# Moving vector units, the early lists and the choice of experts among the chunks of a scan kernel

## The reference

```python
xn = layernorm(x)
dt = softplus(xn @ W_dt1.T @ W_dt2.T + b_dt2)         # [b, t, d]
A_bar = exp(dt * A)                                   # [b, t, d, n], n = 0..15
h = A_bar * h + (A_bar - 1) / A * xn * (xn @ W_B.T)   # along t
y = sum_n h * (xn @ W_C.T)
x = x + y + D_skip * xn
expert = argmax(softmax(layernorm(x) @ Wr + br))      # one of 8 for each token
x = x + gelu(layernorm(x) @ W1[expert] + b1[expert]) @ W2[expert] + b2[expert]
```

## Time and profile before

| | us |
|---|---|
| three runs: median (lowest, highest) | 726.48 (724.77, 732.52) |
| the profiled execution, its own time | 726.01 |
| its span in the trace | 724.3 |
| chunk 4 (first scan to the next chunk's first scan) | 52.8 |
| chunk 5 | 54.1 |
| chunk 6 | 51.9 |
| chunk 7 (to the end of its last scan) | 57.5 |
| from there to the end | 279.3 |

### The profile page before, as it was taken

The page is one execution under the profiler, slowest core; times in us unless marked ns, Lnnn a source line. Parts: engine busy times, 40 slices in busy tenths (PEclk is TensorE's granted clock), DMA queues, the critical chain, the costliest instruction groups (busy, mean ns, idle before and its releaser), DMA issues.

```text
span 724.3 us, 17510 instructions
## 1 busy us (share of the span) xinstructions
PE 682.5 (94%) x5826; PEld 574.6 (79%) x5827; DVE 538.0 (74%) x950; ACT 482.6 (67%) x1005; POOL 485.6 (67%) x616
## 2 busy tenths in 40 slices
PE   8899799999999998899998989999999999999997
PEld 7777677777787776678776778898999999977776
DVE  7799889989989989999999878887343333344441
ACT  3887999998998997899998586433232323233451
POOL 3889998998998987989989587233343434343331
PEclk9699999999999999999999799999999999999999
DMA  6787542342343243143242077711111111111010
GB/s 235 269 258 254 204 145 78 104 148 93 108 152 117 82 137 107 60 148 117 83 125 88 30 256 240 277 41 49 58 52 59 48 58 45 58 38 33 25 45 16
DMA packets 42290, 82.21 MB, mean 114 GB/s; under 512 B 4824, under 2 KB 12637, under 8 KB 42208
## 3 DMA queue, kind: packets, MB, share of 16 engines
q1 hardware_dynamic: 37600, 68.58, 28.7%
q0 software_dynamic: 4608, 12.59, 5.4%
HBM read 69.35 MB, written 13.37 MB: 114 GB/s over the span
## 4 chain that ended last, share of the span: by engine, by line
PE 58%; ACT 12%; POOL 9%; issue 7%; DVE 2%; DMA 1%; SPq 0%; POOLq 0%; ACTq 0%; DVEq 0%
PE WW L1172 16%; PE misc L1209 15%; PE WW L1055 10%; POOL w_sb L667 7%; PE YY L1093 7%; ACT w_sb L835 5%; ACT Csb L825 5%; PE misc L1204 2%; PE WW L1166 2%; DMA w_sb<-c_rows 1%; PE YY L1141 1%; PE misc L969 1%; ACT xin L805 1%; PE misc L981 1%; DVE w_sb L1336 1%
## 5 line engine op out<-in xcount | busy, mean ns | idle before, releaser
L667 POOL TENSOR_TENSOR w_sb<-w_sb,Csb 128x512 f32<-128x512 f32 x224 | 282.7, 1275 | 41.9 <-DVE w_sb L1336 37.7
L1055 PE MATMUL WW<-b_sb,xin 64*128 64x130 f32 (+2 forms) x2304 | 203.3, 293 | 23.4 <-DVE w_sb L1336 12.5
L1055 PEld LDWEIGHTS WW<-b_sb,xin 64*128 64x128 f32 x2304 | 168.4, 192 | 70.3 <-issue 30.6
L1336 DVE TENSOR_TENSOR_SCAN w_sb<-WW,hlast,w_sb 128x512 f32<-128x512 f32 x170 | 210.1, 1269 | 13.5 <-issue 6.5
L835 ACT ACTIVATE w_sb<-dt,negA 128x512 f32<-128x512 f32 x256 | 169.5, 709 | 4.0 <-DVE w_sb L1336 2.0
L916 ACT ACTIVATE dt<-WW,b1c 128x128 f32<-128x128 f32 x256 | 72.8, 387 | 129.2 <-PE WW L1172 129.0
L1093 PE MATMUL YY<-sm,w_sb 128*128 128x128 f32 x1024 | 142.4, 284 | 6.2 <-DVE row L1384 4.3
L729 POOL DMA_INDIRECT y_out<-CbX,ocol x36 | 42.6, 1184 | 142.0 <-DVE CbX L1758 137.3
L1093 PEld LDWEIGHTS YY<-sm,w_sb 128*128 128x128 f32 x1024 | 113.4, 143 | 21.2 <-issue 4.3
L825 ACT ACTIVATE Csb<-w_sb,invA 128x512 f32<-128x512 f32 x150 | 102.5, 713 | 23.2 <-POOL w_sb L667 21.5
L1209 PE MATMUL misc<-w_sb,dt 128*128 x512 | 115.7, 379 | 0.5 <-issue 0.5
(11 more groups left out here) (304 smaller groups left out, 817.7 us busy)
## 6 DMA issues: line engine op xcount, KB each, us to landing
w_sb<-c_rows SPq DMA_DIRECT2D x86, 256.0 KB, 3.3
CbX<-c_rows SPq DMA_DIRECT2D x42, 256.0 KB, 3.3
w_sb<-w_in SPq DMA_DIRECT2D x20, 512.0 KB, 5.7
token_rows<-row SPq DMA_DIRECT2D x8, 1024.0 KB, 4.6
w_sb<-w_in SPq DMA_DIRECT2D x24, 256.0 KB
...
```

Source lines behind the costliest of these rows:

```text
L667: eng.tensor_tensor(hc[g % NHC], hb_of(g), Csb[i % NCS][:, :], ALU.mult).then_inc(s_hcp, 1)
L1055: return eng.matmul(to[:, a:a + width], x_rows[rows, k, h * P:(h + 1) * P], band[rows, k, at:at + width], start=start, stop=not start, ski ...
L1336: eng.tensor_tensor_scan(hb_of(g) if pooled(g) else w_of(g), w_of(g), A[g % NA], hlast[(q - 1) % 2][:, h * N + n:h * N + n + 1] if q % NC ...
```

## The change

- `VECTOR_UNITS`: chunk 4 has the vector unit 5 alone (before: 5 and 12), chunk 5 has 14 (before: 8), chunk 6 none (before: 8), chunk 7 has 6, 11 and 15 (before: 4, 10 and 15). That is 14 in all where 16 were.
- The four parts of `choose` for chunks 0 to 3 go from the end of chunk 4 to the gaps behind the scans 0 and 1 of chunk 5; `rank` goes from PE's unit 0 to unit 2 there, and `place_tokens` is cut in three, behind the items 4, 5 and 6, where it stood behind item 2. The hops, the softplus, the logits and `u` of chunk 5 come a half unit to a unit later.
- In chunk 7 `early1` is filled at PE's units 3 and 4 (before 6 and 7), through `misc[0]`, and `u` at 6 and 7 (before 3 and 4); DVE takes the early list at item 9 (before 17) and `u` at 15 and 16 (before 9 and 11). The steps of `first_table` stand one behind each of the scans 0 to 4 (before: behind 1, 1, 2, 2 and 3).
- The gathers of the first three tiles go from POOL's units 9, 11 and 13 to 7, 9 and 11; the three weight loads from behind the C row of unit 9 to one each behind those of 11, 12 and 13.

```diff
-VECTOR_UNITS = [(4, 8, 12)] + [(5, 12)] * 4 + [(8,)] * 2 + [(4, 10, 15)]
+VECTOR_UNITS = [(4, 8, 12)] + [(5, 12)] * 3 + [(5,), (14,), ()] + [(6, 11, 15)]
...
-ODD = ("u01", "xn0", "bcd", "dt2_0", "dt2_1", "rank", "spread", "early0", "early1")
+ODD = ("u01", "xn0", "bcd", "dt2_0", "dt2_1", "rank", "spread", "early0")
...
         if q == BATCHES[0][1] + 1:
-            at |= {0: [("rank", BATCHES[0][1] - 1)]}
+            at = {1: [("cbt", q)], 2: [("rank", BATCHES[0][1] - 1)], 4: [("xn0", q + 1), ("xn1", q + 1)], 5: [("bcd_a", q + 1)],
...
     else:
-        at = {1: [("cbt", q)], 3: [("u_a", q)], 4: [("u01", q), ("u23", q)], 6: [("early1_a", q)], 7: [("early1", q)],
...
+        at = {1: [("cbt", q)], 3: [("early1_a", q)], 4: [("early1", q)], 6: [("u_a", q)], 7: [("u01", q), ("u23", q)],
...
-                    if q == NQ - 1 and n == 9:
+                    if q == NQ - 1 and n in (11, 12, 13):
                         eng.wait_ge(s_full, HOP["early1", q] + 1)
-                        for i in range(17, 20):
-                            load_weights(i)
+                        load_weights(n + 6)
...
-                    if last and n in (9, 11, 13):
-                        t = (9, 11, 13).index(n)
+                    if last and n in (7, 9, 11):
+                        t = (7, 9, 11).index(n)
                         gather(t, t, 0)
...
-                        if (j, gap) == ((24, 0) if last else (26, 0)):
+                        if (j, gap) == ((28, 1) if late_rank else (26, 0)):
                             logits(q - 1)
...
-                    if (j, gap) in (((9, 1), (11, 1)) if last else ((30, 0), (31, 0))):
-                        u_times_x(q, int(j in (11, 31)))
-                    if q == BATCHES[0][1] and j > 29:
-                        choose(0, 2 * j + gap - 60)
-                    if q == BATCHES[0][1] + 1 and j == 2:
-                        place_tokens(0, (gap,))
+                    if (j, gap) in (((15, 1), (16, 1)) if last else ((31, 0), (31, 1)) if late_rank else ((30, 0), (31, 0))):
+                        u_times_x(q, gap if late_rank else int(j in (16, 31)))
+                    if late_rank and j < 2:
+                        choose(0, 2 * j + gap)
+                    if late_rank and gap and j in (4, 5, 6):
+                        place_tokens(0, (j - 4,))
...
-                    if last and 0 <= 2 * j + gap - 2 <= 4:
-                        first_table(2 * j + gap - 2)
-                    if last and (j, gap) == (17, 0):
+                    if last and gap and j <= 4:
+                        first_table(j)
+                    if last and (j, gap) == (9, 0):
                         keep_ids()
```

More of the change, by code:

```diff
@@ L863, in emit @@
                         copy_first_W1()
-                    if not first and n == (13 if last else 14):
+                    if not first and n == (15 if q == BATCHES[0][1] + 1 else 14):
                         softmax_exp(q - 1)
@@ L1428, in choose, with place_tokens @@
                     eng.tensor_tensor(onehot[:, 0:tiles, :], over_e(top), less8, ALU.is_equal).then_inc(s_oh, 1)
-            def place_tokens(batch, parts=(0, 1)):
+            def place_tokens(batch, parts=(0, 1, 2)):
                 q0, q1 = BATCHES[batch]
@@ L1535, in emit @@
             def emit(q):
-                first, last = q == 0, q == NQ - 1
+                first, last, late_rank = q == 0, q == NQ - 1, q == BATCHES[0][1] + 1
                 def between(j, gap):
```

28 lines of the change are left out of this document (17 added, 11 removed).

## The result

The changed kernel is 0.9% slower: 734.72 us median (730.67 to 735.57, 4 runs) against 726.61 us (724.77 to 732.52, 4 runs) of the kernel before in the same job. The ratio is 1.0088, with a 95% interval of 1.0046 to 1.013. The forecast was 721.4 us and its range ended at 727.5.

The account below looks back on a forecast made before the run. DVE was taken to bound chunks 5 and 6, PE to pace most of chunk 4, and waits to lengthen chunk 7. Chunks 4 to 7 gave -2.2 + 2.0 - 1.0 - 3.4 = -4.6 us on 726.0: 721.4, range 716.5 to 727.5.

Parts of the forecast that it names:

- unit 12's 1.4 us: Chunk 4: two products and the column leave DVE, 1.4 us, mostly lost because the gain stands behind a wait for PE.
- PE's hops move by a unit: Chunk 5: hops shift on PE, with no price of their own in the chunk's +2.0 us.
- needs scan 5 of the chunk anyway: Chunk 5: the unit input queued behind `rank` on PE needs that scan regardless; no cost was given.
- The vector unit's wait of 0.50 us: Chunk 5: a wait ahead of the moved unit's first scan, of the kind seen in chunk 6, 0.50 us.
- Rival 1: Clock falls in chunk 5 where the choice went, kernel slower than before: 726.4 us, or 728.2; chance 0.15.
- POOL's hole of 2.20 us: Chunk 6: POOL's idle time during the old vector unit, to be filled with 2.6 us of work.
- rival 2: POOL becomes the bound: chunk 6 at +1.0, chunk 4 at -0.7, total 724.9 us; chance 0.18.
- The -1.0: Chunk 6: gain taken in us, between bounds -1.9 (DVE alone) and +1.0 (POOL's work and waits).
- -3.4: Chunk 7: -1.6 us for the wait for `u` and -1.8 for SP's late C row; bounds -6.7 and -1.0.
- rival 4: Chunk 7: moving `u` does nothing, its reader still waits 2 us though the clock holds; 723.0 us, chance 0.08.
- far from the table: Chunk 7: `u` moved behind `early1`, away from the table, its wait falling from 1.96 to 0.4 us.
- The C row's 1.8 us: Chunk 7: two waits of unit 10 for a row SP kept back go, -1.8 us.

Follow-up runs that it names:

- e2: Kernel before with only the change's moved choice, rank, placing and chunk-5 hops with their readers: 731.32 us, ratio 1.0053.
- e13: e6 with choice, rank and placing moved, chunk-5 hops as before, 48 more idle products at unit 2 of chunk 5: 726.68 us, ratio 1.0005.
- e10: e6 with chunk 5's hops and their readers shifted as in the change, choice, rank and placing as before: 726.34 us, ratio 1.0013.
- e14: e5 with chunk 5's hops and their readers as before, placing behind items 4 and 5, 48 more idle products: 728.51 us, ratio 1.0042.
- e5: The whole change with idle products, whose result nobody reads, in PE's waits of chunks 5 and 7: 728.91 us, ratio 1.0027.
- e11: e6 with the change's moved choice, rank, placing and chunk-5 hops with their readers: 728.26 us, ratio 1.004.
- e9: e6 with choice and rank moved, placing behind items 4 and 5, chunk 5's hops as before: 728.15 us, ratio 1.003.
- e6: Kernel before with idle products, whose result nobody reads, in PE's waits of chunks 5 and 7: 724.84 us, ratio 0.9988.
- e12: Kernel before with the change's chunk-7 part, idle products in chunk 5 as in e6 and chunk 7 as in e5: 723.05 us, ratio 0.9978.

## Why the prediction was wrong

**Chunk 4: right in its mechanism, -2.8 us for -2.2.** The choice counted in full (-2.6 in e2 and e13, forecast 2.5) and unit 12's 1.4 us were lost but for 0.2, because PE paces the chunk, as the prediction had it. POOL did not bound it: it was busy 48.8 us there, not the 50.8 of the sum, since the work spilled over. Its last product of the chunk ended 1.7 us into chunk 5, where before it had ended 0.35 us ahead of it.

**Chunk 5: here the prediction failed, +7.4 us for +2.0.** The failed step is "PE's hops move by a unit", which stood in the sum without a price; alone it costs 3.4 us (e10), of which an estimated 1.7 is the place of the hops and as much a short fall of the clock. `rank` was also taken as free, since the unit behind it "needs scan 5 of the chunk anyway". That named who is queued behind `rank` on PE, but not who waits for its result: DVE, for 0.94 us. The vector unit's wait of 0.50 us, expected once, came three times in e14, where the unit is at 14 and the hops are back. The choice's own work was right (2.4 for 2.5 us, less the 1.3 us of slack, which did not help: DVE's idle time in the change is 5.7 us of 61.4). The same chunk's DVE busy time came as foreseen, 55.8 us for 55.

**Rival 1 occurred, and does not explain chunk 5 by itself.** The clock fell for 10.24 us where and as it said. But in e5 and e11 the chunk is as long without that fall, with one of 3.41 us at 313 or 314 in its place. In the change DVE was busy 10.02 of 10.30 us during the long fall, which can have covered much of it. Where nothing else was late (e9 against e13) the fall cost 3.1 us, which confirms its price. What the change's chunk 5 takes without any fall was not measured: every kernel with its hops has one there.

**Chunk 6: wrong sign, +0.8 us at full clock and +2.4 with a fall, for -1.0.** POOL's hole of 2.20 us was filled as foreseen, and what followed was rival 2, 52.7 us where it gives 52.9. That the figures meet so nearly is luck in part: rival 2 has POOL busy for 52.1 us, and in e5 it is busy 50.8 and idle 2.0. The -1.0 was taken between bounds with no row behind it; the row of 0.50 us said that POOL was already as late as it may be, so without the vector unit the wait could repeat, as it did in three units. Neither rival had it that POOL's lateness reaches PE through ACT and brings the clock down.

**Chunk 7: the total holds at full clock only, the terms don't, +0.6 us for -3.4.** At full clock the change's chunk 7 takes 54.03 us for 54.1 forecast. That this agrees is luck. `u` waits 1.12 us for 0.4 forecast (and for the 2 of rival 4), and the list, to which the sum gave nothing, 0.82; against that the waits ahead of scans, which the sum left as they were, fell from 3.8 us (1.54, 1.42, and one of 0.80 at 422.63 that the earlier trace rows and the sum leave out) to 2.2 (0.66, 0.31 and 1.24 in e5). The one left out, before:

```profile
422.63 2.46 DVE L1336 TENSOR_TENSOR_SCAN w_sb<-WW,hlast,w_sb 128x512 f32<-128x512 f32 x2 [0.80 <-issue]
```

As the kernel ran, the premise that `u` stands "far from the table" helped the wrong hop: `early1` took its place in the slow stretch and waited 4.91 us. Spreading the table did not hold the clock: PE had 4.84 us of work in the 7.00 ahead of the fall, and waited 0.34 and 1.70 us in them. The C row's 1.8 us went as forecast. And the -3.4 was measured from a chunk 7 with a slow clock: 2.3 us of it are to be had in the old order by keeping PE busy (e6), and the order itself is worth 0.5 (e12).

**The rest** was 0.5 us shorter, at the edge of what was allowed. It comes with the chunk-7 part: the eight kernels that have it take 278.59 to 278.90 us from the last scan to the end, the eight others 279.15 to 279.33. Which of its steps does it was not tried.

**The range** ended at 727.5 because rivals 1 and 2 were made alternatives. They occurred together, but even both at their highest, 728.2 + 3.5 = 731.7 us, fall 3.0 short of 734.7: the hops were in none of them. With the falls removed that idle products remove, the terms come to -2.8 + 7.9 + 0.8 - 1.2 - 0.6 = +4.1 us (e5 less e6, chunks 4 to 7 and the rest), and those falls take 4.0 more from the change than from the kernel before (5.4 less 1.4).

The fastest kernel of the study is e12, the part for chunk 7 alone with idle products: 0.9978 of the kernel before (0.996 to 0.9995), 723.05 us in six runs.
